# Rework of the Haar and mixer stages of a small vision tower: what VectorE, ScalarE and GpSimd each do

## The chip, the cores and the metric

The kernel runs on one core of one Trainium2 chip. The metric is the device time of one execution in microseconds: the median of three runs before the change is 135.28 us (134.98 to 137.23).

## The reference, cut to what matters

The input is eight images of 256 by 256 (fp32). Three blocks follow one another:

```python
# 1. wavelet block: three Haar levels down, weights, three levels up
cur = img
for _ in range(3):
    cur, h, v, d = _dwt2(cur); details.append((h, v, d))
rec = cur * sigmoid(cur.reshape(B, -1) @ Wa + ba)[:, :, None]
for (h, v, d), (Wd, bd) in zip(reversed(details), det_params):
    w = softmax(stack([h, v, d], 1).reshape(B, -1) @ Wd + bd)
    rec = _idwt2(rec, h * w[:, 0], v * w[:, 1], d * w[:, 2])
h = rec
# 2. mixer, on x = layernorm(h)
delta = softplus(x @ Wdelta + bdelta);  B_bar = delta * (x @ Wb + bb)
A_cum = clip(cumsum(delta * -softplus(A), axis=1), -20, 20)
state = exp(A_cum) * cumsum(B_bar * exp(-shifted(A_cum)), axis=1)
h = h + state @ Wc + bc + x @ Wd + bd
# 3. quantised FFN, on x = layernorm(h): 8-bit rounding by maxima of x, of each
#    weight row and of silu(gate) * up, which are taken over whole tensors
h = h + ffn(x)
```

## The kernel before, in words

The eight images form two halves of four. A half lies on 128 partitions (image and row strip) with eight rows of 256 on each. Every engine has its instructions in one order that is written out by hand; semaphores join them. There is no scheduler: an engine stands still at the first instruction whose wait isn't met, and all that is behind it stands too.

VectorE makes the Haar sums and differences of the first half (`analyse_level`, L898 for the step down the rows) and of the second (`down_second`). TensorE transposes the bands, makes the dots with the weights, and makes the logits of the softmax. `shifted_logits` and `band_weights` are a chain of tiny VectorE instructions around an exponential on ScalarE. `synthesise_level` goes up again, from level 2 to level 0: at each level four scaled sums (L974 and L977) make a column step out of average and horizontal, vertical and diagonal detail, and two sums (L981, L983) join them. ScalarE scales only the vertical detail (L740). Moments follow (L987), then row normalisation, shared by ScalarE (L770) and VectorE (L1002).

TensorE transposes the normalised rows; ScalarE copies them out of PSUM (L781); TensorE projects them (L540) and makes the direct part of the mixer (L556). ScalarE makes the softplus. VectorE makes the step sizes (L1042), a scan over time for the logarithmic decay (L1056, L1060), the state's input (L1049), then a product, a scan and a product for the state (L1066, L1067, L1070). GpSimd adds the mixer's biases once the state is there (L395). VectorE takes the maxima of the FFN's weights (L1027) and their scales between the states of the two halves; ScalarE rounds the weights (L749) and GpSimd clamps them. `keep_warm` matmuls on TensorE have no use but to keep it busy. VectorE then adds the mixer's result, normalises, takes the maximum of the whole tensor, and the FFN runs.

## Time and profile before

| What | Value |
|---|---|
| Median of the runs (range) | 135.28 us (134.98 to 137.23) |
| Profiled execution, its span | 135.05 us, 133.3 us |
| Busy: VectorE, TensorE, ScalarE, GpSimd | 119.4, 105.8, 74.5, 31.4 us |
| Chain that ended last: VectorE, TensorE, issue | 62%, 24%, 5% |
| Mean granted clock of TensorE | 0.947 |
| Haar stage, mixer, second normalisation and maximum, FFN (about) | to 46, to 68, to 85, to 133 us |

The profile comes from one execution. An instruction's duration is from its start to its end; independent instructions on one engine overlap by about a tenth of a microsecond, so a run of equal ones is shorter than count times duration. The chain that ended last is followed back from the last instruction: at each step to what released it. The granted clock is 1.00 for 2.4 GHz and 0.50 for 1.2 GHz.

### The profile page before, as it was taken

To read this page: it belongs to the slowest core of one execution; us is meant where nothing else is said; L and a number is where in the kernel's file an instruction comes from. 1 tells how busy PE (TensorE), PEld (TensorE's weight loads), DVE (VectorE), ACT (ScalarE), POOL (GpSimd) and SP (SyncE) were. 2 spreads that over 40 slices of the span, in tenths; PEclk is the share of its full clock that TensorE was granted. 3 is DMA by queue.
4 is the path that set the end of the run, shared out by engine and by line. 5 is a ranking of instruction groups with operands and counts; after the bars stand their busy time and mean duration, and the time that the engine had idled before them with its cause. 6 is when DMAs were issued, how large, how long until landed. Compare 5 with 4: busy or idle time off the path is not lost.

```text
span 133.3 us, 1778 instructions
## 1 busy us (share of the span) xinstructions
PE 105.8 (79%) x589; PEld 70.5 (53%) x589; DVE 119.4 (90%) x250; ACT 74.5 (56%) x145; POOL 31.4 (24%) x46
## 2 busy tenths in 40 slices
PE   0588979993989988799999329689999993996830
PEld 0577967993753856548889103144344331764410
DVE  0599978999979999999997999788999998999992
ACT  3204324421795139678943949369999921997000
POOL 6400000001000000490369700007767730000000
PEclk9999999999599999999999975799999999999995
DMA  3999950000000000000230390029000000003354
GB/s 87 362 421 306 417 224 7 0 0 0 0 0 0 7 0 0 0 0 0 50 68 5 76 163 0 0 46 174 17 0 0 7 0 0 0 33 125 121 194 157
DMA packets 10938, 10.21 MB, mean 77 GB/s; under 512 B 8370, under 2 KB 8626, under 8 KB 10802
## 3 DMA queue, kind: packets, MB, share of 16 engines
q1 hardware_dynamic: 10642, 9.59, 23.5%
q10 hardware_dynamic: 288, 0.52, 1.1%
q8 instruction: 4, 0.07, 0.2%
q14 instruction: 4, 0.03, 0.1%
HBM read 6.05 MB, written 2.10 MB: 61 GB/s over the span
## 4 chain that ended last, share of the span: by engine, by line
DVE 62%; PE 24%; issue 5%; DMA 3%; POOL 2%; ACT 2%; DVEq 0%
PE bank L608 13%; DVE stats L987 4%; DVE early L1208 4%; PE bank L427 4%; DVE state_mem L1204 4%; DVE wabs L1027 4%; DVE xmax L1084 3%; DVE middle L1197 3%; DVE early L977 3%; DVE early L974 3%; PE bank L487 3%; DVE h L1078 3%; DMA early<-in_x 3%; DVE middle L898 2%; POOL h L395 2%
## 5 line engine op out<-in xcount | busy, mean ns | idle before, releaser
L608 PE MATMUL bank<-state_mem,wqT 128*128 128x512 bf16 x80 | 17.7, 380 | 0.5 <-DVE state_mem L1163 0.5
L420 POOL TENSOR_TENSOR early<-raw,state_mem 128x512 f32<-128x512 f32 x10 | 13.0, 1296 | 19.1 <-ACT raw L871 19.1
L432 PE MATMUL bank<-restart,ident 128*128 128x512 bf16 x39 | 12.7, 472 | 4.8 <-DVE xmax L1084 4.8
L395 POOL TENSOR_TENSOR h<-h,bias_rows 128x512 f32<-128x512 f32 x8 | 9.9, 1274 | 24.7 <-DVE state_mem L1070 24.7
L864 ACT ACTIVATE state_mem<-bank,gscale 128x512 f32<-128x512 f32 x22 | 14.4, 700 | 1.1 <-PE bank L608 0.8
L621 PE MATMUL bank<-wqT,middle 128*128 128x256 bf16 (+1 forms) x96 | 12.6, 274 | 2.5 <-DVE middle L1197 2.4
L556 PE MATMUL bank<-mixer_w,early 128*128 128x256 f32 x64 | 14.5, 382 | 0.0
L1173 DVE TENSOR_REDUCE amax<-early 128x1 f32<-128x1024 f32 x11 | 13.2, 1212 | 0.4 <-POOL early L420 0.4
L556 PEld LDWEIGHTS bank<-mixer_w,early 128*128 128x128 f32 x64 | 11.9, 190 | 2.6 <-issue 1.1
L770 ACT ACTIVATE early<-h,nmr,rstd 128x256 f32<-128x256 f32 x23 | 11.9, 589 | 1.8 <-DVE nmr L995 1.8
L608 PEld LDWEIGHTS bank<-state_mem,wqT 128*128 128x128 bf16 x80 | 7.3, 98 | 10.5 <-DVE early L1181 1.8
L877 ACT ACTIVATE raw<-early,ainv 128x512 int16<-128x512 f32 x16 | 9.9, 710 | 5.0 <-DVE ainv L1193 5.0
L621 PEld LDWEIGHTS bank<-wqT,middle 128*128 128x128 bf16 (+1 forms) x96 | 8.3, 97 | 7.1 <-DVE middle L1197 4.4
L722 ACT ACTIVATE early<-bank 128x512 f32<-128x512 f32 x8 | 4.4, 598 | 12.2 <-PE bank L427 12.2
L987 DVE BATCH_NORM_STATS2 stats<-h 128x6 f32<-128x512 f32 x16 | 10.6, 695 | 0.3
L432 PEld LDWEIGHTS bank<-restart,ident 128*128 128x128 bf16 x39 | 4.4, 118 | 10.2 <-DVE xmax L1084 5.0
L487 PE MATMUL bank<-wT,early 128*128 128x96 f32 x48 | 9.2, 352 | 0.0
L1181 DVE SCALAR_TENSOR_TENSOR early<-bank,gscale,state_mem 128x512 f32<-128x512 f32 x12 | 8.9, 745 | 0.1
L649 PE MATMUL bank<-ident 128*128 128x128 f32 x20 | 4.6, 428 | 4.9 <-DMA early<-in_x 4.9
L540 PE MATMUL bank<-early,mixer_w 128*64 128x512 f32 x32 | 7.4, 599 | 1.2 <-ACT early L781 1.2
L487 PEld LDWEIGHTS bank<-wT,early 128*128 128x128 f32 x48 | 8.0, 205 | 0.1
L763 ACT ACTIVATE var<-stats,eps 128x8 f32<-128x8 f32 x4 | 1.2, 304 | 12.2 <-DVE stats L987 12.2
(144 smaller groups left out, 207.3 us busy)
## 6 DMA issues: line engine op xcount, KB each, us to landing
out<-early SPq DMA_DIRECT2D x7, 256.0 KB, 2.5
early<-in_x SPq DMA_DIRECT2D x1, 1024.0 KB, 8.9
wT<-in_dot_weights SPq DMA_DIRECT2D x1, 784.0 KB, 6.9
raw<-in_gate_rows SPq DMA_DIRECT2D x1, 768.0 KB, 11.1
raw<-in_up_rows SPq DMA_DIRECT2D x1, 768.0 KB, 12.4
raw<-in_down_rows SPq DMA_DIRECT2D x1, 768.0 KB, 13.7
early<-in_x ACTq DMA_DIRECT2D x2, 256.0 KB, 4.8
early<-in_x SPq DMA_DIRECT2D x2, 256.0 KB, 4.7
```

The costliest lines, as they stand in the source:

```text
L395: nc.gpsimd.tensor_tensor(rows, rows, bias.unsqueeze(1).to_broadcast([P, 2, C]), ALU.add).then_inc(biased, 1)
L420: nc.gpsimd.tensor_tensor(act[:, u, :], up_s[:, m % UPS, :], silu[:, u % SIL, :], ALU.mult).then_inc(pool_act_ready, 1)
L432: nc.tensor.matmul(into[:, :], ident16[:, :], restart[:, 0:PAIR // 2].bitcast(bf16), start=True, stop=True)
L487: nc.tensor.matmul(own(half, 0)[:, 0:3 * S], bandT[:, half, 4 * b + r, :], wT1[:, b, :, r::4], start=(m + r == 0), stop=(m == 2 and r == 3 ...
L556: nc.tensor.matmul(own(half, MIX[n])[:, i * C:(i + 1) * C], xnT[:, half, c, (2 * n + i) * P:(2 * n + i + 1) * P], wd_t[:, c, :], start=(i ...
L608: last = nc.tensor.matmul(dst[:, :], w, xqT[:, k, :, c, :], start=(c == 0), stop=(c == CH - 1))
L621: return nc.tensor.matmul(down_bank(n, i)[:, i * C:(i + 1) * C], act_q[rows, unit_of[t, k], q * P:(q + 1) * P], wdT[rows, t, :], start=sta ...
L770: nc.scalar.activation(xn[:, half, r, :], h[:, half, r, :], ACT.Identity, bias=nmr[:, norm, half, r:r + 1], scale=rstd[:, norm, half, r:r ...
L864: nc.scalar.activation(silu[:, u % SIL, :], bank[2 * (u % 3)][:, :], ACT.Silu, scale=gscale[:, 0, t:t + 1]).then_inc(silu_ready, 1)
L877: nc.scalar.activation(act_i[:, u, :], act[:, u, :], ACT.Copy, scale=ainv[:, :]).then_inc(acti_ready, 1)
L987: last = nc.vector.bn_stats(stats[:, norm, half, 2 * n:2 * n + 2, :].rearrange("p r k -> p (r k)"), h[:, half, 2 * n:2 * n + 2, :].rearran ...
L1173: nc.vector.tensor_reduce(amax[:, m:m + 1], act[:, 2 * m:2 * m + 2, :].rearrange("p a t -> p (a t)"), AX.X, ALU.max, apply_absolute_value= ...
```

## The change

It rewrites the first two blocks in several places and moves small pieces between engines.

- Sums of the analysis and of the second half's row step are joined or parted differently: one instruction covers both outputs of `down`, and the four sums of `down_second` stand in another order.
- The softmax chain is shorter: twelve logits with pads, the image weight's sign in the mask, no negated weights, the average scaled in one instruction. The small constants of the limits are made on GpSimd.
- At level 1 of both halves and level 0 of the second (`PRESCALED`), ScalarE scales the horizontal and diagonal details too; VectorE then makes the column step by one sum and one difference over both parts. At the other levels the four scaled sums stay, with the subtraction in the operator.
- On ScalarE the second half's small products stand ahead of the first two copies of transposed rows, and its level 0 products ahead of the last two.
- In the mixer the clipped sum comes from one scan per image with a limit, the decay is the exponential of its differences, and the state is a scan that adds and multiplies. Of the second half VectorE normalises four rows, not two, and copies two of four transposed tiles out of PSUM; ScalarE copies the others.
- Four `keep_warm` matmuls go, and the second half's transposes and projections stand ahead of the last direct bank.
- Of the weight scales VectorE keeps the reciprocal; GpSimd makes the rest, behind the first half's biases.
- The two quantisations of activations multiply by two scalars at once instead of making a scale first.

Core of the diff:

```diff
+        PRESCALED = ((1,), (1, 0))
...
+                pool.wait_ge(wabs_ready, 1)
+                nc.gpsimd.tensor_scalar(winv[:, :, :], wabs_inv[:, :, :], QMAX, None, ALU.mult).then_inc(winv_ready, 1)
+                nc.gpsimd.tensor_scalar(wscale[:, :, :], wabs[:, :, :], 1.0 / QMAX, None, ALU.mult).then_inc(wscale_ready, 1)
+                pool.wait_ge(wscale_ready, 1)
+                for c in range(CH):
+                    last = nc.gpsimd.tensor_scalar(diag[:, c, :], ident[:, :], wscale[:, 2, c:c + 1], None, ALU.mult)
+                last.then_inc(diag_ready, 1)
...
                 if half == 1:
+                    weight_scales()
                     clamp_weights(0)
                 add_bias(half)
...
             projections(0)
             mix_direct(0, (0, 1, 2))
-            keep_warm(WARM_PROJECT, own(1, 3))
-            xn_transposed(1, GROUPS[1][0])
+            for g in GROUPS[1]:
+                xn_transposed(1, g)
+            projections(1)
             mix_direct(0, (3,))
-            xn_transposed(1, GROUPS[1][1])
-            projections(1)
             mix_state(0, range(R // 2))
...
                 for n in levels:
-                    nc.scalar.activation(vband[n][:, half, :], band[n][:, half, V_, :], ACT.Copy,
-                                         scale=wts[:, half, 3 * n + 1:3 * n + 2]).then_inc(v_ready, 1)
+                    dst = vband2[:, half, :] if n == 2 else coarse[n][:, 1, :]
+                    nc.scalar.activation(dst, band[n][:, half, V_, :], ACT.Copy,
+                                         scale=wts[:, half, 3 * n + 1:3 * n + 2]).then_inc(v_ready[n], 1)
+                    if n in PRESCALED[half]:
+                        for k, b in ((0, H_), (1, D_)):
+                            nc.scalar.activation(detail[n][:, k, :], band[n][:, half, b, :], ACT.Copy,
+                                                 scale=wts[:, half, 3 * n + 2 * k:3 * n + 2 * k + 1]).then_inc(detail_ready[n], 1)
...
             def decays(half):
-                sc.wait_ge(alog_ready, half + 1)
-                v = lambda t: t[:, half, :].rearrange("p (a t) -> p a t", t=T)
-                nc.scalar.activation(v(edn)[:, :, 1:T], v(alog)[:, :, 0:T - 1], ACT.Exp, scale=-1.0).then_inc(edn_ready, 1)
-                nc.scalar.activation(eup[:, half, :], alog[:, half, :], ACT.Exp).then_inc(eup_ready, 1)
+                if half == 0:
+                    sc.wait_ge(acol_ready, 1)
+                sc.wait_ge(dlog_ready, half + 1)
+                nc.scalar.activation(decay[:, half, :], dlog[:, half, :], ACT.Exp,
+                                     scale=acol[:, 4:5]).then_inc(decay_ready, 1)
...
-            normalise(0, 0, range(ACT_ROWS[0] - 1))
+            normalise(0, 0, ACT_ROWS[0][:-1])
             softmax_exp(1)
-            normalise(0, 0, (ACT_ROWS[0] - 1,))
+            normalise(0, 0, ACT_ROWS[0][-1:])
+            scale_vertical(1, (2, 1))
             xn_out(0, (0,))
-            scale_vertical(1, (2, 1))
+            scale_vertical(1, (0,))
             xn_out(0, (1,))
-            scale_vertical(1, (0,))
             softplus(0)
             inverse_std(0, 1)
-            normalise(0, 1, range(R // 2))
+            normalise(0, 1, ACT_ROWS[1])
+            xn_out(1, (0, 1))
             decays(0)
-            normalise(0, 1, range(R // 2, ACT_ROWS[1]))
-            xn_out(1, (0, 1))
             softplus(1)
             quantise_weights(0)
...
-                vert = vband[n][:, half, :].rearrange("p (r c) -> p r c", c=width)
-                for odd, w in enumerate((wts, wneg)):
-                    stt(dst[:, 0, odd::2, :], bandv[:, H_, :, :], w[:, half, 3 * n:3 * n + 1], avg, ALU.mult, ALU.add)
-                dve.wait_ge(v_ready, 3 * half + 3 - n)
-                for odd, w in enumerate((wts, wneg)):
-                    step = seq.mark(stt(dst[:, 1, odd::2, :], bandv[:, D_, :, :], w[:, half, 3 * n + 2:3 * n + 3], vert,
-                                        ALU.mult, ALU.add))
+                if n in PRESCALED[half]:
+                    parts = coarse[n][:, :, :].rearrange("p k (r c) -> p k r c", c=width)
+                    details = detail[n].rearrange("p k (r c) -> p k r c", c=width)
+                    dve.wait_ge(v_ready[n], half + 1)
+                    dve.wait_ge(detail_ready[n], 2 * (half + 1 if n else half))
+                    tt(dst[:, :, 0::2, :], parts, details, ALU.add)
+                    step = seq.mark(tt(dst[:, :, 1::2, :], parts, details, ALU.subtract))
+                else:
+                    vert = (vband2[:, half, :] if n == 2 else coarse[n][:, 1, :]).rearrange("p (r c) -> p r c", c=width)
+                    for odd, op in enumerate((ALU.add, ALU.subtract)):
+                        stt(dst[:, 0, odd::2, :], bandv[:, H_, :, :], wts[:, half, 3 * n:3 * n + 1], avg, ALU.mult, op,
+                            reverse1=odd == 1)
+                    dve.wait_ge(v_ready[n], half + 1)
+                    for odd, op in enumerate((ALU.add, ALU.subtract)):
+                        step = seq.mark(stt(dst[:, 1, odd::2, :], bandv[:, D_, :, :], wts[:, half, 3 * n + 2:3 * n + 3], vert,
+                                            ALU.mult, op, reverse1=odd == 1))
...
+            def second_turned(m):
+                g = GROUPS[1][m]
+                dve.wait_ge(xnT_psum, 4 + 2 * m + CH)
+                nc.vector.tensor_copy(xnT[:, 1, CH - 1, 4 * g * P:4 * (g + 1) * P],
+                                      own(1, 2 * g + CH - 1)[:, :]).then_inc(xnT_ready, 1)
...
             def log_decay(half):
                 dve.wait_ge(delta_ready, half + 1)
-                seq.link(nc.vector.tensor_tensor_scan(csum[:, :], restart[:, :], delta[:, :], 0.0,
-                                                      ALU.mult, ALU.add))
                 if half == 0:
-                    dve.wait_ge(acol_ready, 1)
-                ts(alog[:, half, :], csum[:, :], acol[:, 4:5], -20.0, ALU.mult, ALU.max).then_inc(alog_ready, 1)
+                    dve.wait_ge(limit_ready, 1)
+                    dve.wait_ge(consts, 1)
+                for q in range(B // 2):
+                    step = seq.mark(nc.vector.tensor_tensor_scan(csum[:, q, 1:T + 1], delta[:, q * T:(q + 1) * T],
+                                                                 limit[:, 0:1].to_broadcast([P, T]), 0.0, ALU.add, ALU.min))
+                seq.wait(step)
+                tt(dlog[:, half, :].rearrange("p (q t) -> p q t", t=T), csum[:, :, 1:T + 1], csum[:, :, 0:T],
+                   ALU.subtract).then_inc(dlog_ready, 1)
             def state(half):
-                dve.wait_ge(edn_ready, half + 1)
+                dve.wait_ge(decay_ready, half + 1)
                 dve.wait_ge(bbar_ready, half + 1)
-                seq.link(tt(bsh[:, :], bbar[:, half, :], edn[:, half, :], ALU.mult))
-                seq.link(nc.vector.tensor_tensor_scan(hs[:, :], restart[:, :], bsh[:, :], 0.0,
-                                                      ALU.mult, ALU.add))
-                dve.wait_ge(eup_ready, half + 1)
-                tt(hT[:, half, :], eup[:, half, :], hs[:, :], ALU.mult).then_inc(hT_ready, 1)
+                for q in range(B // 2):
+                    cut = slice(q * T, (q + 1) * T)
+                    last = nc.vector.tensor_tensor_scan(hT[:, half, cut], bbar[:, half, cut], decay[:, half, cut], 0.0,
+                                                        ALU.add, ALU.mult)
+                last.then_inc(hT_ready, 1)
...
-            down_second(ALU.add, A_).then_inc(bands[1], 1)
+            down_second(ALU.add, A_, 0)
+            down_second(ALU.add, A_, 1).then_inc(bands[1], 1)
             own_strips(0)
-            down_second(ALU.subtract, H_).then_inc(bands[1], 1)
+            down_second(ALU.subtract, H_, 0)
             shifted_logits(0)
+            down_second(ALU.subtract, H_, 1).then_inc(bands[1], 1)
...
-            normalise_rows(0, 0, range(ACT_ROWS[0], R))
+            normalise_rows(0, 0, DVE_ROWS[0][:2])
             shifted_logits(1)
+            limits()
+            normalise_rows(0, 0, DVE_ROWS[0][2:])
...
             centre(0, 1)
+            normalise_rows(0, 1, DVE_ROWS[1])
+            state_input(0)
+            for m in range(2):
+                second_turned(m)
             log_decay(0)
-            state_input(0)
-            normalise_rows(0, 1, range(ACT_ROWS[1], R))
+            weight_maxima(0)
             state(0)
-            weight_maxima(0)
             weight_maxima(1)
```

Two places show the moved order. On ScalarE, from the second half's softmax to the softplus (`early<-bank` is the copy of transposed rows, the rows with `wts` are the scaled details), before:

```order
L734 ACTIVATE ez<-zc 128x10 [waits z_ready]
L770 ACTIVATE early<-h,nmr,rstd 128x256 [waits nmr_ready]
L781 ACTIVATE early<-bank 128x512 [waits xnT_psum] x2
L740 ACTIVATE middle<-middle,wts 128x32 [waits wts_ready]
L740 ACTIVATE middle<-middle,wts 128x128
L781 ACTIVATE early<-bank 128x512 [waits xnT_psum] x2
L740 ACTIVATE middle<-middle,wts 128x512 [waits wts_ready]
L790 ACTIVATE state_mem<-bank,cols 128x512 [waits proj_done]
```

and in the changed kernel:

```order
L767 ACTIVATE ez<-zc 128x12 [waits z_ready]
L808 ACTIVATE early<-h,nmr,rstd 128x256 [waits nmr_ready]
L774 ACTIVATE middle<-middle,wts 128x32 [waits wts_ready]
L774 ACTIVATE early<-middle,wts 128x128
L778 ACTIVATE early<-middle,wts 128x128 x2
L819 ACTIVATE early<-bank 128x512 [waits xnT_psum] x2
L774 ACTIVATE early<-middle,wts 128x512 [waits wts_ready]
L778 ACTIVATE early<-middle,wts 128x512 x2
L819 ACTIVATE early<-bank 128x512 [waits xnT_psum] x2
L828 ACTIVATE state_mem<-bank,cols 128x512 [waits proj_done]
```

Four products stand ahead of the first copies, three of 512 elements ahead of the last ones.

On VectorE, from the row normalisation of the second half to its step sizes (`state_mem` holds the mixer's tensors, `wabs` the weight maxima), before:

```order
L1002 TENSOR_SCALAR early<-h,rstd,nmr 128x256 x2
L1066 TENSOR_TENSOR state_mem<-state_mem 128x512
L1067 SCALAR_TENSOR_TENSOR state_mem<-restart,state_mem 128x512
L1070 TENSOR_TENSOR state_mem<-state_mem 128x512
L1027 TENSOR_REDUCE wabs<-raw 128x6 x2
L1027 TENSOR_REDUCE wabs<-raw 128x2
L1032 TENSOR_SCALAR wscale<-wabs 128x18
L1033 RECIPROCAL winv<-wscale 128x18
L1035 TENSOR_SCALAR diag<-ident,wscale 128x128 x2
L1042 TENSOR_TENSOR state_mem<-state_mem 128x512
```

and in the changed kernel:

```order
L1056 COPY early<-bank 128x512 x2
L1096 SCALAR_TENSOR_TENSOR state_mem<-state_mem,limit 128x256 x2
L1099 TENSOR_TENSOR state_mem<-state_mem 128x512
L1068 TENSOR_REDUCE wabs<-raw 128x6
L1108 SCALAR_TENSOR_TENSOR state_mem<-state_mem 128x256 x2
L1068 TENSOR_REDUCE wabs<-raw 128x6
L1068 TENSOR_REDUCE wabs<-raw 128x2
L1073 RECIPROCAL wabs_inv<-wabs 128x18
L1079 TENSOR_TENSOR state_mem<-state_mem 128x512
```

Two copies out of PSUM now stand ahead of the scans, one weight maximum stands between scans and state, and the scales are gone from VectorE. The scans read SCALAR_TENSOR_TENSOR in this listing.

## Rows read from the trace of the kernel before

**Rows 1.** Chain that ended last, shares of the span by engine.

```profile
DVE 62%; PE 24%; issue 5%; DMA 3%; POOL 2%; ACT 2%; DVEq 0%
```

**Rows 2.** Timeline of VectorE, 9 to 23 us: start, duration (us), instruction, [idle before].

```profile
9.09 1.43 DVE L898 TENSOR_TENSOR middle<-early 128x256 f32<-128x256 f32 x4
...
15.61 1.29 DVE L926 TENSOR_TENSOR middle<-early 128x512 f32<-128x512 f32 x2
...
17.75 0.49 DVE L936 TENSOR_TENSOR picked<-bank,strip_mask 128x320 f32<-128x320 f32 x1 [0.71 <-PE bank L498]
18.27 0.49 DVE L938 TENSOR_REDUCE part<-picked 128x10 f32<-128x320 f32 x1
...
20.84 0.18 DVE L958 RECIPROCAL rden<-den 128x4 f32<-128x4 f32 x1
...
22.98 0.35 DVE L974 SCALAR_TENSOR_TENSOR early<-middle,wts,early 128x128 f32<-128x128 f32 x1
```

**Rows 3.** Timeline of TensorE, the second matmul of the first half's logits.

```profile
19.20 0.39 PE L509 MATMUL bank<-bias,ones 1*128 1x10 f32 x2
```

**Rows 4.** Timeline of VectorE, 33 to 44 us.

```profile
33.04 0.49 DVE L938 TENSOR_REDUCE part<-picked 128x10 f32<-128x320 f32 x1
...
33.64 1.38 DVE L1002 TENSOR_SCALAR early<-h,rstd,nmr 128x256 f32<-128x256 f32 x4
...
37.11 0.25 DVE L974 SCALAR_TENSOR_TENSOR early<-middle,wts,avg 128x32 f32<-128x32 f32 x1
...
38.09 0.25 DVE L977 SCALAR_TENSOR_TENSOR early<-middle,wts 128x32 f32<-128x32 f32 x1 [0.57 <-ACT middle L740]
...
40.91 0.75 DVE L974 SCALAR_TENSOR_TENSOR early<-middle,wts,early 128x512 f32<-128x512 f32 x1
...
43.68 1.23 DVE L981 TENSOR_TENSOR h<-early 128x1024 f32<-128x1024 f32 x1
```

**Rows 5.** Timeline of ScalarE: vertical products, copies out of PSUM, weight rounding.

```profile
37.75 0.60 ACT L740 ACTIVATE middle<-middle,wts 128x32 f32<-128x32 f32 x2
38.25 1.07 ACT L781 ACTIVATE early<-bank 128x512 f32<-128x512 f32 x2
39.20 0.73 ACT L740 ACTIVATE middle<-middle,wts 128x512 f32<-128x512 f32 x1
...
60.41 2.51 ACT L749 ACTIVATE raw<-raw,winv 128x256 int16<-128x256 f32 x6 [0.34 <-DVE winv L1033]
```

**Rows 6.** Timeline of TensorE, 39 to 55 us: projections, direct part, transposes.

```profile
39.46 3.67 PE L540 MATMUL bank<-early,mixer_w 128*64 128x512 f32 x16 [0.45 <-ACT early L781]
43.07 5.45 PE L556 MATMUL bank<-mixer_w,early 128*128 128x256 f32 x24
...
53.85 1.04 PE L427 MATMUL bank<-ident,early 128*128 128x128 f32 x8
```

**Rows 7.** Windows of TensorE: stretch, length, busy (instructions), granted clock, DMA share, GB/s.

```profile
31.30:33.50 2.20, 0.00 (x1) 1.00 0.00 0
33.70:37.10 3.40, 3.40 (x15) 0.51 0.00 0
...
78.40:85.00 6.60, 5.75 (x14) 0.50 0.25 31
```

**Rows 8.** Timeline of VectorE in the mixer, 49 to 68 us.

```profile
49.27 1.22 DVE L1056 TENSOR_TENSOR_SCAN state_mem<-restart,state_mem 128x512 f32<-128x512 f32 x1
...
54.22 0.69 DVE L1070 TENSOR_TENSOR state_mem<-state_mem 128x512 f32<-128x512 f32 x1
54.82 4.93 DVE L1027 TENSOR_REDUCE wabs<-raw 128x6 f32<-128x1536 f32 x3
...
64.97 0.68 DVE L1066 TENSOR_TENSOR state_mem<-state_mem 128x512 f32<-128x512 f32 x1
...
66.94 0.69 DVE L1070 TENSOR_TENSOR state_mem<-state_mem 128x512 f32<-128x512 f32 x1
```

**Rows 9.** Timeline of GpSimd, the first half's bias.

```profile
55.08 4.96 POOL L395 TENSOR_TENSOR h<-h,bias_rows 128x512 f32<-128x512 f32 x4 [21.58 <-DVE state_mem L1070]
```

192 lines of the change are left out of this document (100 added, 92 removed).

## The prediction

> **What bounds the kernel now.** I read the chain of waits first: VectorE holds 62% of it [rows 1], so a VectorE instruction that goes away counts, unless the engine was about to wait there. Then the timeline of each engine around the change. In the Haar stage VectorE waits only twice: 0.71 us for the first half's dots and 0.57 us for ScalarE's scaled vertical detail [rows 2, 4]. From 38 to 67 us it runs without a gap while TensorE and ScalarE deliver ahead of it [rows 5, 6, 8]. The reader is to see that the cover is thin: TensorE's projections begin the moment ScalarE's last copy of the transposed rows ends [rows 5, 6], and what is queued on ScalarE ahead of those copies moves TensorE.
>
> **Stage 1, up to the first half's image.** The four 256-element sums of an analysis step take 1.43 us and two of 512 take 1.29 [rows 2]: 0.14 us less, twice before TensorE may start, once each at the two coarse levels. TensorE's chain starts 0.28 us sooner; the rest ends in the 0.71 us wait. From the strip sum (end 18.76) to level 1 (22.98) it is 4.22 us now [rows 2]. After: the sum ends at 18.48, the logits follow 0.83 us later as now [rows 2, 3], maximum, shift and latencies take 0.40, and the second half of the sums (0.61, half of the 1.29 pair) covers the exponential, up to 20.31. Four dependent tiny steps at about 0.18 each [rows 2] less overlap give 0.65, level 2 its old 1.17 (two tiers of small instructions that don't change): level 1 starts at 22.13, 0.85 sooner. There, two sums of 256 (0.79, from the 256-element pace of 0.34) replace four scaled sums (0.35 each less overlap, 1.17 [rows 2]): 0.38. ScalarE's four small products at 0.25 to 0.30 [rows 5] end near 21.9, before they are wanted; it was idle then. Together 1.23 us at the first half's image, and level 0, whose form is new only in the operator, follows at its old price.
>
> **Stage 2, the second half's image.** From the strip sum's end (33.53) to level 2 (37.11) it is 3.58 us [rows 4]. After, counted from 32.30: maximum and shift lie between two pairs of row normalisations, the exponential waits for ScalarE's third row (34.0), and the tiny steps start when the fourth VectorE row has passed; level 2 starts at 34.88, after 2.58: 1.00 us. The vertical product is no longer behind ScalarE's copies, so the 0.57 us wait and its latency go (0.66 with the step's own spacing), and level 1 gives 0.38 again. VectorE stands at level 0 at 37.64 instead of 40.91 [rows 4].
>
> Now ScalarE. From the weights (34.70): four small products, 1.1 us; two copies out of PSUM, 1.0; then the vertical, horizontal and diagonal products of 512 at 0.61 apart, the last 0.73 long [rows 5]. The last ends at 38.78. VectorE waits **1.14 us** for it. Two sums of 1024 (2.41, from 1.23 each less overlap) replace four scaled sums (2.77 [rows 4]): 0.36. The image is 3.27 - 1.14 + 0.36 = 2.5 us sooner, and moments with it.
>
> Here a rule speaks against the change. The row: 512 elements scaled on ScalarE take 0.73 us, the scaled sum on VectorE 0.75, adding included [rows 4, 5]; so at level 0 three ScalarE products save 0.36 us of VectorE and cost 1.14 of waiting, while at level 1 the same exchange is free because ScalarE has nothing else to do. The Trainium skill ("ScalarE: Activation LUTs", Rules for kernel authors) says multiplications belong on VectorE rather than ScalarE; by it alone every prescaled level would lose, by the rows only the widest does.
>
> **Stage 3, the mixer.** ScalarE's two last copies (1.07 [rows 5]) now end at 39.8 instead of 39.3. TensorE: projections 3.61 (39.46 to 43.07) and three direct banks, 5.45 less overlap [rows 6], to 48.7; then all sixteen transposes of the second half, 0.13 each: 50.75. The four keep-warm matmuls between are gone, which only lets the transposes follow directly. VectorE passes step sizes and centring at 46.8 (49.27 less 2.5 [rows 8]), its four rows (1.38 [rows 4]) and the state input (0.75) at 48.9, and must now copy the second channel half of both groups out of PSUM: it waits, in sum some **1.4 us**, and the last copy (0.6, below the 0.69 of a 512-element sum [rows 8]) ends at 51.35. Behind it queue the scans: two of 256 (half of 1.22 each [rows 8], 1.26 together) and a difference (0.69): 53.35. The exponential lies under the first weight maximum (a third of 4.93 [rows 8]); the new state is two scans, 1.27, in place of product, scan, product (2.66 [rows 8]). State 0 ends at 56.3, **1.4 us later** than now (54.91 [rows 8]), with one weight maximum done early.
>
> From there to state 1 VectorE needs 10.15 us now (54.82 to 64.97 [rows 8]). After: 1.65 less for that maximum, 0.6 less for weight scales given to GpSimd, 0.3 more because scans and difference take 1.98 and not 1.66: 8.2, so 64.5. GpSimd, however, comes to the scales only after adding the bias (4.96 [rows 9]) behind state 0: 61.45. Its 18-element scale shows nowhere; I take 0.3, bounds 0.1 and 0.7. Six weight tiles on ScalarE (2.51 [rows 5]) stand ahead of the second exponential (at most 0.73): 65.0. So state 1 waits 0.5 us and ends at 66.3 against 67.63 (66.94 plus 0.69 [rows 8]): 1.35 sooner. TensorE's second direct part is then still running, as now, and the transposes of the weights leave SP's queue up to 1.5 us later, long before the FFN uses them.
>
> The two quantisations each lose one dependent tiny step on VectorE (0.12 and 0.11). The twelve-wide logits, the memsets, the fourth mask, the limits on GpSimd at 17 us lie beside other work; if they did not, it would be tenths. **Sum: 1.6 us, 133.45** against the profiled execution's 135.05.
>
> **TensorE's clock.** That sum needs the full clock. After 2.2 us without work the clock stood at half for 3.4 us (33.7 to 37.1), and after a longer pause from 78.4 to 85.0 [rows 7]. The change shortens the first pause (31.0 to 32.35 instead of 33.58), but between the last keep-warm matmul (near 36.95) and projections at 39.8 opens a new one of 2.9 us, with nothing to fill it. I expect it to fall there once. At half clock 3.4 us do 1.7 us of work, so the price lies between 0 and 1.7; part of the low stretch may fall into the pause, so I take 1.0. VectorE waits for the transposes, so all of it passes on. **Forecast: 134.5 us.** The median of the runs shown, 135.28, is 0.23 above the profiled execution, which is within their spread; I leave the forecast there.
>
> **The rivals.**
> - *The clock holds.* For it: a shorter pause of 1 us earlier in the trace left it alone, and if it still falls at 33 us the keep-warm matmuls run longer and close the second pause. Against: 2.2 us sufficed once. Time 133.45, 0.8 either way.
> - *The clock stays low for long*, as from 78.4 to 85.0 [rows 7]. Place: projections and direct mixing of the first half. Price 3.3 us; it decides the sign from 1.6 us on. Time 136.8, slower than before. Against it: that stretch began after 4 us of pause, and the work here is dense.
> - *ScalarE is late at both levels.* If the small products come after the level-2 step in both halves, level 1 gains nothing (0.76), and if the 512-element products don't overlap, level 0 waits 0.36 more: 135.6 with the fall. For it: 0.25 us spacing has one row only; against: it has 0.6 us to spare in the first half. The rule of the Trainium skill named above points this way.
>
> **How the numbers follow.** Forecast 0.45 (133.9 to 135.2), clock holds 0.30, late ScalarE 0.12, long low clock 0.10, something unseen 0.03. The range 132.5 to 136.5 leaves out the low end of the second case and the top of the fourth. A difference under 2% (below 132.57 or above 137.99) is what a measurement of this kernel can't well tell from none. Only the clock case with a cheaper PSUM copy gets below: 0.14. Only the long low clock with a late GpSimd gets above: 0.04. Within: 0.82.
>
> **What would show it.** In the changed profile: level 1 as two sums under 0.45 us each without a wait; a wait of about 1 us on ScalarE's diagonal product before the second half's level 0; a pause of near 3 us before the projections, and the granted clock there; VectorE's PSUM copies waiting for TensorE; state 0 later and state 1 sooner than now; a short wait of state 1 for the exponential. I am wrong if VectorE's PSUM copies don't wait, or if the second state comes later than 67.6 us.

## The result, and the profile after

The change makes the kernel slower by 0.9%: 137.43 us (median of 20 executions, 135.7 to 141.68) against 136.76 us (20, 134.64 to 138.79) for the kernel before on the same chip. The ratio is 1.0094, with a 95% interval of 1.0056 to 1.0132. (The ratios here come from undisturbed executions alone, so they can differ a little from those of the medians, and four traces below, those without prescaled level 0 in the changed kernel, with the earlier rounding, with GpSimd's sums and without any prescaling, come from slower executions.) The forecast was 134.5 us, the range 132.5 to 136.5, and the sign was a gain of 0.6% on 135.28. The profiled execution took 135.96 us, its span 134.2 (before 135.05 and 133.3): 0.91 us more.

The chain that ended last, by engine, answers [rows 1]:

```profile
DVE 44%; PE 31%; ACT 8%; issue 7%; POOL 5%; DMA 3%; DVEq 0%; POOLq 0%
```

VectorE holds 44% of it and not 62%. TensorE has 31% and not 24%, ScalarE 8% and not 2%, GpSimd 5% and not 2%: more work that lay beside VectorE is now waited for.

**The Haar stage.** VectorE, from the first half's level 1 to the second half's moments, answers [rows 2, 4] (start, duration in us, instruction, idle before and who ended it):

```profile
22.01 0.42 DVE L1010 TENSOR_TENSOR early<-early 128x256 f32<-128x256 f32 x1
22.35 0.42 DVE L1011 TENSOR_TENSOR early<-early 128x256 f32<-128x256 f32 x1
...
35.17 0.41 DVE L1015 SCALAR_TENSOR_TENSOR early<-middle,wts,avg 128x32 f32<-128x32 f32 x2
...
39.06 1.23 DVE L1010 TENSOR_TENSOR early<-early 128x1024 f32<-128x1024 f32 x1 [1.17 <-ACT early L778]
...
43.90 2.51 DVE L1029 BATCH_NORM_STATS2 stats<-h 128x6 f32<-128x512 f32 x4
```

Level 1 starts at 22.01 (22.98 before) as two sums of 0.42 without a wait; the second half's level 2 at 35.17 (37.11). Level 0 waits 1.17 us for ScalarE's diagonal product. The moments end at 46.41, 2.17 us sooner than before. Of this 0.23 us is chance: the first sums of the images began at 4.58 us here and at 4.81 before, and in the other kernels below at 4.58 to 5.12, once at 6.33.

**TensorE's clock**, which answers [rows 7] (stretch, length, busy time and instructions of TensorE's matmuls, its weight loads, VectorE, ScalarE and GpSimd, then granted clock, DMA share, GB/s):

```profile
30.80:32.20 1.40, 0.00 (x0) 0.00 (x0) 1.36 (x4) 0.51 (x2) 0.72 (x1) 1.00 0.00 0
32.30:37.40 5.10, 5.10 (x22) 4.57 (x23) 4.52 (x21) 4.64 (x12) 0.00 (x0) 0.51 0.00 0
37.40:39.20 1.80, 1.80 (x6) 0.46 (x4) 0.63 (x3) 1.80 (x4) 0.00 (x0) 0.50 0.00 0
...
40.04:43.71 3.67, 3.67 (x17) 1.34 (x17) 3.64 (x4) 1.69 (x3) 0.00 (x0) 1.00 0.00 0
```

The clock fell after the pause of 1.46 us before 32.26, not at the projections. The transposes and keep-warm matmuls then ran at half clock to 39.36, and only 0.68 us was idle before the projections at 40.04, which ran at the full clock in the 3.67 us they had before.

**The mixer.** VectorE from the first half's step sizes (L1079) over the copies out of PSUM (L1056) to the state of the second half (L1108), answers [rows 8]:

```profile
46.32 0.68 DVE L1079 TENSOR_TENSOR state_mem<-state_mem 128x512 f32<-128x512 f32 x1
...
50.00 0.69 DVE L1056 COPY early<-bank 128x512 f32<-128x512 f32 x1 [0.73 <-PE bank L462]
50.88 0.69 DVE L1056 COPY early<-bank 128x512 f32<-128x512 f32 x1 [0.18 <-PE bank L462]
51.48 1.26 DVE L1096 TENSOR_TENSOR_SCAN state_mem<-state_mem,limit 128x256 f32<-128x256 f32 x2
...
55.05 1.26 DVE L1108 TENSOR_TENSOR_SCAN state_mem<-state_mem 128x256 f32<-128x256 f32 x2
...
59.70 1.07 DVE L1079 TENSOR_TENSOR state_mem<-state_mem 128x512 f32<-128x512 f32 x1
60.81 2.23 DVE L1096 TENSOR_TENSOR_SCAN state_mem<-state_mem,limit 128x256 f32<-128x256 f32 x2
...
65.72 2.03 DVE L1108 TENSOR_TENSOR_SCAN state_mem<-state_mem 128x256 f32<-128x256 f32 x2
```

The same three steps cost more in the second half than in the first: the step-size sum 1.07 against 0.68, the decay scans 2.23 against 1.26, the state scans 2.03 against 1.26: 2.1 us in all. State 0 ends at 56.31, state 1 at 67.75 (67.63 before): of the 2.17 us nothing is left. GpSimd in that stretch answers [rows 9]. The first row holds the third and fourth bias addition together, the second row the fourth alone:

```profile
58.95 2.95 POOL L419 TENSOR_TENSOR h<-h,bias_rows 128x512 f32<-128x512 f32 x2
60.17 1.73 POOL L419 TENSOR_TENSOR h<-h,bias_rows 128x512 f32<-128x512 f32 x1
...
61.99 0.55 POOL L425 TENSOR_SCALAR winv<-wabs_inv 128x18 f32<-128x18 f32 x1
62.51 0.60 POOL L426 TENSOR_SCALAR wscale<-wabs 128x18 f32<-128x18 f32 x1
63.21 1.61 POOL L429 TENSOR_SCALAR diag<-ident,wscale 128x128 f32<-128x128 f32 x2
65.16 1.47 POOL L436 TENSOR_SCALAR raw<-raw 128x1536 bf16<-128x1536 int16 x1 [0.34 <-ACT raw L787]
```

The fourth addition, 60.17 to 61.90, took 1.73 us; four took 4.96 before. VectorE's scans started in it at 60.81. The state scans started at 65.72 in the clamp of 65.16 to 66.63. Before the change the additions (55.08 to 60.04) lay beside VectorE's three weight maxima (54.82 to 59.75), which read one operand.

ScalarE in that stretch:

```profile
62.57 2.51 ACT L787 ACTIVATE raw<-raw,winv 128x256 int16<-128x256 f32 x6 [5.63 <-POOL winv L425]
64.98 0.71 ACT L839 ACTIVATE state_mem<-state_mem,acol 128x512 f32<-128x512 f32 x1
```

It rounds the weights (L787) once GpSimd's 18-element scale is there, and makes the exponential (L839) behind that. The exponential ended at 65.69, so state 1 couldn't have started before 65.69 even with quick decay scans.

**The last stage.** From the first rounding (85.20; 85.35 before) to the maximum of the products it is 26.60 us and not 26.04. VectorE and GpSimd there, of the changed kernel:

```profile
90.60 1.54 DVE L1206 TENSOR_SCALAR state_mem<-state_mem 128x1024 bf16<-128x1024 int16 x1
...
90.59 1.27 POOL L455 TENSOR_TENSOR early<-raw,state_mem 128x512 f32<-128x512 f32 x1 [14.70 <-ACT raw L909]
```

and of the kernel before:

```profile
90.64 0.43 DVE L1158 TENSOR_SCALAR state_mem<-state_mem 128x1024 bf16<-128x1024 int16 x1
...
90.68 1.51 POOL L420 TENSOR_TENSOR early<-raw,state_mem 128x512 f32<-128x512 f32 x1 [14.91 <-ACT raw L871]
```

The same two instructions meet. Whichever starts first, here by 0.01 and there by 0.04 us, keeps its time; the other is stretched. From the second rounding to the last sum it is 0.63 us longer too (18.93 against 18.30). Seven instructions that now multiply by two scalars take 0.54 and 0.41 us where they took 0.48 and 0.35, which makes 0.4; the other 0.2 is a wait for TensorE, which the run with one scalar explains below.

### The profile page after: what moved, and what is told of

Same layout as the page of the kernel before. It is cut to its first block, busy times and chain, and to the rows that moved or that the text cites. A ratio compares the mean times of both kernels' runs of the same rounds, so it can differ in the third digit from the quotient of the medians.

```text
span 134.2 us, 1765 instructions
## 1 busy us (share of the span) xinstructions
PE 106.5 (79%) x585; PEld 71.3 (53%) x585; DVE 119.3 (89%) x227; ACT 74.3 (55%) x146; POOL 35.6 (27%) x59
## 4 chain that ended last, share of the span: by engine, by line
DVE 44%; PE 31%; ACT 8%; issue 7%; POOL 5%; DMA 3%; DVEq 0%; POOLq 0%
PE bank L642 11%; DVE early L1255 4%; PE bank L590 4%; POOL h L419 4%; DVE state_mem L1251 4%; PE bank L462 4%; DVE h L1118 4%; DVE xmax L1124 3%; PE bank L655 3%; PE bank L522 3%; DVE stats L1029 3%; DMA early<-in_x 3%; PE bank L574 3%; DVE middle L935 2%; DVE middle L1244 2%
## 5 line engine op out<-in xcount | busy, mean ns | idle before, releaser
L467 PE MATMUL bank<-restart,ident 128*128 128x512 bf16 x35 | 12.0, 494 | 7.0 <-DVE xmax L1124 7.0
L419 POOL TENSOR_TENSOR h<-h,bias_rows 128x512 f32<-128x512 f32 x8 | 10.4, 1329 | 25.5 <-DVE state_mem L1108 25.5
L655 PE MATMUL bank<-wqT,middle 128*128 128x256 bf16 (+1 forms) x96 | 13.9, 297 | 1.7 <-DVE middle L1244 1.7
L655 PEld LDWEIGHTS bank<-wqT,middle 128*128 128x128 bf16 (+1 forms) x96 | 9.2, 105 | 6.7 <-DVE middle L1244 3.3
L808 ACT ACTIVATE early<-h,nmr,rstd 128x256 f32<-128x256 f32 x21 | 10.9, 589 | 1.8 <-DVE nmr L1037 1.8
L787 ACT ACTIVATE raw<-raw,winv 128x256 int16<-128x256 f32 x12 | 5.0, 495 | 5.6 <-POOL winv L425 5.6
```

Source lines behind the costliest of these rows:

```text
L419: nc.gpsimd.tensor_tensor(rows, rows, bias.unsqueeze(1).to_broadcast([P, 2, C]), ALU.add).then_inc(biased, 1)
L467: nc.tensor.matmul(into[:, :], ident16[:, :], restart[:, 0:PAIR // 2].bitcast(bf16), start=True, stop=True)
L655: return nc.tensor.matmul(down_bank(n, i)[:, i * C:(i + 1) * C], act_q[rows, unit_of[t, k], q * P:(q + 1) * P], wdT[rows, t, :], start=sta ...
L808: nc.scalar.activation(xn[:, half, r, :], h[:, half, r, :], ACT.Identity, bias=nmr[:, norm, half, r:r + 1], scale=rstd[:, norm, half, r:r ...
```

## The experiments

The theory: what was to be won is lost where GpSimd's work lies beside VectorE instructions that read two operands from SBUF (**A**). The first rival: the new scans are slow in the second half by themselves (**B**).

**The scales back on VectorE.**

```diff
-                    weight_scales()
...
+                seq.link(ts(wscale[:, :, :], wabs[:, :, :], 1.0 / QMAX, None, ALU.mult))
+                nc.vector.reciprocal(winv[:, :, :], wscale[:, :, :]).then_inc(winv_ready, 1)
+                for c in range(CH):
+                    last = ts(diag[:, c, :], ident[:, :], wscale[:, 2, c:c + 1], None, ALU.mult)
```

> The changed kernel with the weight scales back on VectorE (0.66 us more there), nothing else. Theory A, GpSimd and VectorE hinder each other when VectorE reads two SBUF operands: the second half's decay scans (2.23 us for two in the changed kernel, 1.26 in the first half) fall to between 1.3 and 1.8 us since only the end of the bias additions still lies beside them, the state scans (2.03) stay slow where the clamping of the gate weights reaches them and else fall to 1.26, and state 1 ends 0.6 to 1.2 us sooner than 67.75; 0.5 to 1.0 us off the time of the changed kernel. Theory B, the new scans are slow by themselves in the second half: they stay at 2.2 and 2.0 us, and the time rises by 0.5 us.

Measured: 137.62 us (6 executions), ratio 1.0156 [1.0001, 1.0312]. VectorE, then GpSimd:

```profile
59.40 0.72 DVE L1072 TENSOR_SCALAR wscale<-wabs 128x18 f32<-128x18 f32 x1
...
60.34 1.25 DVE L1075 TENSOR_SCALAR diag<-ident,wscale 128x128 f32<-128x128 f32 x2
...
62.22 1.27 DVE L1099 TENSOR_TENSOR_SCAN state_mem<-state_mem,limit 128x256 f32<-128x256 f32 x2
63.53 1.77 DVE L1102 TENSOR_TENSOR state_mem<-state_mem 128x512 f32<-128x512 f32 x1
...
67.21 1.26 DVE L1111 TENSOR_TENSOR_SCAN state_mem<-state_mem 128x256 f32<-128x256 f32 x2
...
56.36 4.95 POOL L419 TENSOR_TENSOR h<-h,bias_rows 128x512 f32<-128x512 f32 x4 [24.10 <-DVE state_mem L1111]
63.14 1.61 POOL L436 TENSOR_SCALAR raw<-raw 128x1536 bf16<-128x1536 int16 x1 [1.84 <-ACT raw L786]
```

The scans are back at 1.27 and 1.26, with GpSimd idle beside them: B falls. But the time didn't come back, which A had expected: other instructions came to lie beside GpSimd. The scale took 0.72 (0.28 in the kernel before), the diagonal 1.25 (0.39), the difference 1.77 (0.69), ending 0.55 us after the clamp. State 1 ended at 68.47. Moving the cause moved the victim. Scale and diagonal read one tensor and not two, so A is too narrow as it is worded.

**The collision put into the old kernel.** GpSimd gets six instructions of 128x320 with unused results behind its bias additions; VectorE's are untouched.

```diff
+                    pool.wait_ge(winv_ready, 1)
+                    for k in range(6):
+                        seq.link(nc.gpsimd.tensor_scalar(picked[:, k % 2, :, :].rearrange("p j s -> p (j s)"),
+                                                         restart[:, 0:NW * S], 0.5, None, ALU.mult))
                     clamp_weights(0)
```

> The kernel before the change, with one thing added: behind the first half's bias additions GpSimd multiplies the strip mask by 0.5 six times (128x320 each, results not used), from the moment the weight scales are there (about 60.4 us) until about 63 us, beside VectorE's step-size sum and scan of the second half, whose instructions stay as they were. Theory A (a VectorE instruction that reads two operands from SBUF is held up while GpSimd works): in the second half the step-size sum takes about 1.0 us instead of 0.68 or the old scan about 2 instead of 1.22, in all 1.0 us more; state 1 ends about 1 us later, near 68.6; time about 0.7 us over the kernel before, less what the clock's phase hides. Theory B (the scans with a limit are slow in the second half for a reason of their own, data or form): the old sum and scan keep 0.68 and 1.22, state 1 ends at 67.6, time unchanged.

The second version differs in GpSimd's instruction alone, a sum of two operands from SBUF in place of a product of one with a constant:

```diff
+                        seq.link(nc.gpsimd.tensor_tensor(picked[:, k % 2, :, :].rearrange("p j s -> p (j s)"),
+                                                         restart[:, 0:NW * S], restart[:, S:(NW + 1) * S], ALU.add))
```

> The kernel before the change, again with six GpSimd instructions of 128x320 added behind the first half's bias additions (results not used), but now sums of two operands from SBUF in place of products of one operand with a constant. With the products the second half's sum, scan and state grew by 0.5 us in all and not by 1.0. Theory A, second form (what holds VectorE is GpSimd's traffic on SBUF, and an instruction with two operands makes more of it): step-size sum 0.69 grows to about 1.0, the scan from 1.35 to about 2.0, product, scan and product of the state together by 0.5 to 1.0 if GpSimd still works then; state 1 ends at 69.0 to 69.5 and not at 68.05. Theory B, second form (only scans with a limit, with their third operand, are held): as with the products, state 1 at 68.0 to 68.2.

With products: 136.26 us (10), ratio 1.0016 [0.9963, 1.0068]. The two scans, and GpSimd:

```profile
61.28 1.35 DVE L1060 TENSOR_TENSOR_SCAN state_mem<-restart,state_mem 128x512 f32<-128x512 f32 x1
...
65.79 1.47 DVE L1071 TENSOR_TENSOR_SCAN state_mem<-restart,state_mem 128x512 f32<-128x512 f32 x1
...
60.53 7.53 POOL L414 TENSOR_SCALAR picked<-restart 128x320 f32<-128x320 f32 x6 [0.52 <-DVE winv L1037]
```

With sums: 139.75 us (4), ratio 1.0200 [1.0107, 1.0293]:

```profile
61.47 1.77 DVE L1060 TENSOR_TENSOR_SCAN state_mem<-restart,state_mem 128x512 f32<-128x512 f32 x1
63.28 0.91 DVE L1064 TENSOR_SCALAR state_mem<-state_mem,acol 128x512 f32<-128x512 f32 x1
...
66.10 1.24 DVE L1070 TENSOR_TENSOR state_mem<-state_mem 128x512 f32<-128x512 f32 x1
67.38 1.77 DVE L1071 TENSOR_TENSOR_SCAN state_mem<-restart,state_mem 128x512 f32<-128x512 f32 x1
69.19 1.77 DVE L1074 TENSOR_TENSOR state_mem<-state_mem 128x512 f32<-128x512 f32 x1
...
60.71 7.36 POOL L414 TENSOR_TENSOR picked<-restart 128x320 f32<-128x320 f32 x6 [0.50 <-DVE winv L1037]
68.15 2.26 POOL L402 TENSOR_SCALAR raw<-raw 128x1536 bf16<-128x1536 int16 x1
```

State 1 ends at 68.05 with the products and 70.96 with the sums, 67.63 without either. So the old scan and products, which the change doesn't touch, slow down beside GpSimd as well: the collision is shown in the old kernel, and B's second form (only scans with a limit) falls. But A's price was wrong by kind. GpSimd worked equally long in both (7.53 and 7.36 us), and the products with a constant cost VectorE 0.45 us where the sums cost 3.2, counted from the step-size sum, some of it (the last product, 1.77 for 0.69) beside the clamp that they pushed back to 68.15. Also wrong in detail: the step-size sum at 60.75 kept its 0.69, and the clip with a scalar, which reads one operand, did grow, from 0.49 to 0.91. State 1 came 1.5 us later than A had expected at most (69.5).

**The new order on VectorE, with the scales there too.** Scans fill the wait for TensorE's transposes, and the one-operand maxima lie beside the bias additions.

```diff
             state_input(0)
+            log_decay(0)
             for m in range(2):
                 second_turned(m)
-            log_decay(0)
-            weight_maxima(0)
             state(0)
+            weight_maxima(0)
             weight_maxima(1)
```

> The changed kernel with the weight scales back on VectorE (as in the first experiment) and VectorE's order in the mixer changed: the first half's step-decay scans stand ahead of the two copies out of PSUM, and all three weight maxima stand behind the first state. So the scans fill the wait for TensorE's transposes, and the maxima, which read one operand, lie beside GpSimd's bias additions. Theory A (GpSimd's work holds VectorE's two-operand instructions): state 0 ends near 53.7 instead of 56.3; the three maxima take 4.9 to 5.0 us; the scales again 0.28 and 0.39, the second half's sum 0.68, its scans 1.26; state 1 ends near 65.4 instead of 67.75; time about 2 us under the changed kernel, 135.0 to 135.7, that is 0.985 to 0.995 of the kernel before. Theory B (the second half's state is bound by something else: ScalarE's rounding of the weights, TensorE, or transfers): state 1 stays at 67 to 68 and the time with it.

Measured: 134.62 us (6; 133.34 to 136.38), ratio 0.9877 [0.9785, 0.9970].

```profile
52.61 1.27 DVE L1111 TENSOR_TENSOR_SCAN state_mem<-state_mem 128x256 f32<-128x256 f32 x2
53.80 4.91 DVE L1067 TENSOR_REDUCE wabs<-raw 128x6 f32<-128x1536 f32 x3
58.75 0.30 DVE L1072 TENSOR_SCALAR wscale<-wabs 128x18 f32<-128x18 f32 x1
...
59.57 0.68 DVE L1082 TENSOR_TENSOR state_mem<-state_mem 128x512 f32<-128x512 f32 x1
60.28 1.27 DVE L1099 TENSOR_TENSOR_SCAN state_mem<-state_mem,limit 128x256 f32<-128x256 f32 x2
...
64.20 1.25 DVE L1111 TENSOR_TENSOR_SCAN state_mem<-state_mem 128x256 f32<-128x256 f32 x2
...
54.05 4.96 POOL L419 TENSOR_TENSOR h<-h,bias_rows 128x512 f32<-128x512 f32 x4 [21.36 <-DVE state_mem L1111]
62.08 1.53 POOL L436 TENSOR_SCALAR raw<-raw 128x1536 bf16<-128x1536 int16 x1 [3.06 <-ACT raw L786]
```

Every VectorE row has its unstretched price, GpSimd's additions 4.96. State 0 ends at 53.88 (expected 53.7), state 1 at 65.45 (65.4; 67.75 in the changed kernel). A holds in its numbers, but the new order does two things. From the moments to state 1 it takes 18.75 us and not 21.34: 2.1 us come from the rows that are no longer stretched, 0.9 from VectorE's waits for the copies, which are gone, and the scales take 0.6 of it back. So the collision is the larger part of what is won here, not all of it.

**Level 0 of the second half without prescaling**, in the changed kernel:

```diff
-        PRESCALED = ((1,), (1, 0))
+        PRESCALED = ((1,), (1,))
```

> The changed kernel without the prescaled details at level 0 of the second half: VectorE makes four scaled sums there again, ScalarE two products of 512 fewer. By the prediction's arithmetic the wait of 1.17 us goes and 0.36 us of VectorE's work comes back: the second half's image 0.8 us sooner, the projections 1.2 us sooner, state 0 at 55.2 to 55.6 instead of 56.3. How much arrives at the end depends on the mixer: 0.8 us if GpSimd's work moves along with state 0, near nothing if TensorE or the clash behind state 0 takes it.

Measured: 135.91 us (12), ratio 1.0004 [0.9929, 1.0080]; the changed kernel has 1.0094, and the intervals overlap. The collision is the same here (step-size sum 1.07, scans 2.23 and 2.03). Counted from the end of the strip sum, the moments end at 13.18 us and not 14.21, state 1 at 34.12 and not 35.55. Level 0 went without a wait through four scaled sums (1.42 and 1.41 for two). So prescaling at the widest level loses 1.0 us there and 1.4 at state 1. In the repaired kernel (new order, scales on VectorE, one scalar, below) the same edit was run again, and then prescaling taken out at level 1 as well (`PRESCALED = ((), ())`):

> As the one before, and level 0 of the second half by four scaled sums again, so that ScalarE scales horizontal and diagonal details at level 1 alone. State 1 ends 0.9 us sooner, near 64.5 (65.35 to 64.48 between the two kernels with all repairs). If the wait in the last stage that ate this there (1.26 us for ScalarE's gate, behind TensorE at half clock) came from the clock's phase, 0.5 to 0.9 us under the one before, about 132.5 to 133.5; if it comes whenever that stage starts sooner, no difference.

> The kernel with the new order, the scales on VectorE, one scalar, and no prescaling at any level: ScalarE scales the vertical details alone, and every column step is four scaled sums. Against the same kernel with level 1 prescaled (first half's level 1 at 22.39 us and two sums of 0.42 each, span 130.3; state 1 ends at 64.50). Theory A (the exchange gains at level 1, where ScalarE has nothing else to do): level 1 takes 1.17 in place of 0.79 in both halves, so the first half's image comes 0.38 later, the second half's 0.76 less what the second half's dots cover; state 1 ends at 65.0 to 65.3; time 0.4 to 0.8 over that kernel, 133.0 to 134.2. Theory B (prescaling is worth nothing at any level, as a rule that keeps products on VectorE would have it): the vertical products come sooner on ScalarE because four others are gone, level 0 and level 1 start sooner or at once, and state 1 ends at 64.5 or earlier.

| Prescaled levels, repaired kernel | Median (executions) | Ratio to before | State 1 ends |
|---|---|---|---|
| 1, and 0 of the second half | 134.80 us (6) | 0.9822 [0.9746, 0.9899] | 65.30 |
| 1 alone | 133.88 us (6) | 0.9831 [0.9759, 0.9903] | 64.51 |
| none | 135.01 us (6) | 0.9818 [0.9678, 0.9959] | 64.84 |

The ratios don't tell the three apart; the traces do. With level 0 prescaled VectorE waits 1.17 us at 39.22; without, it starts at 38.10 and state 1 comes 0.79 sooner; the two profiled executions took 132.91 and 132.06 us. At level 1, VectorE without and with prescaling (the first half's level 2 began 0.38 us later in the second of these executions):

```profile
36.49 0.61 DVE L1014 SCALAR_TENSOR_TENSOR early<-middle,wts,early 128x128 f32<-128x128 f32 x2
37.02 0.61 DVE L1018 SCALAR_TENSOR_TENSOR early<-middle,wts,early 128x128 f32<-128x128 f32 x2
```

```profile
36.50 0.43 DVE L1009 TENSOR_TENSOR early<-early 128x256 f32<-128x256 f32 x1
36.84 0.42 DVE L1010 TENSOR_TENSOR early<-early 128x256 f32<-128x256 f32 x1
```

Four scaled sums reach the row step 1.18 us after their start (36.49 to 37.67), two sums 0.79 (36.50 to 37.29). State 1 ended at 64.84, between what theory A (65.0 to 65.3) and theory B (64.5 or earlier) had expected. It is 0.33 later without prescaling although its first half began 0.38 earlier: together 0.7 for both halves, near the 0.76 of the expectation, provided that the earlier start would have reached the end. So level 1 gains 0.39 us in each half by these rows, and nothing of it can be seen in the time.

**One scalar in the quantisations.** The scale is made first, and one scalar multiplies:

```diff
-                    seq.link(ts(xq_i[:, half, rows, :], xn[:, half, rows, :], gmax1_inv[:, 0:1], limit_den[:, 1:2],
-                                ALU.mult, ALU.mult))
+                    seq.link(ts(xq_i[:, half, rows, :], xn[:, half, rows, :], xinv[:, 0:1], None, ALU.mult))
...
-                    rounded[u] = seq.mark(ts(act_i[:, u, :], act[:, u, :], amax1_inv[:, 0:1], limit_den[:, 2:3], ALU.mult, ALU.mult))
+                    rounded[u] = seq.mark(ts(act_i[:, u, :], act[:, u, :], ainv[:, 0:1], None, ALU.mult))
```

> The changed kernel with both quantisations multiplying by one finished scale again. Theory C, a tensor-scalar instruction with two pointer scalars costs 0.06 us more than with one, and seven of them in the last stage stand on the chain: roundings of 512 elements fall from 0.54 to 0.48 us, and 0.3 to 0.4 us go from the last stage; VectorE's clamp of the third block goes back from 1.54 to 0.43 us if it starts ahead of GpSimd's first multiplication, which takes another 0.4 us. In all 0.4 to 0.8 us faster than the changed kernel. Rival: the saved tiny step is worth more than that, and the time rises by 0.1 to 0.2 us.

Measured: 136.77 us (12), ratio 1.0079 [1.0025, 1.0133], not to be told from 1.0094. In the trace the roundings take 0.75 and 0.48 again, the clamp misses GpSimd's multiplication (0.43), and the first rounding to the maximum is 26.04 us as before the change (26.60 with it). From the second rounding to the last sum it is 18.72 and not 18.93; before 18.30. It isn't back at 18.30 because VectorE waited 0.28 us for TensorE's first product there, at granted clock 0.50 (115 to 118 us). The changed kernel had 0.50 there as well (114.3 to 117.6), and so had both old kernels with added GpSimd work; the old kernel by itself had 1.00. Two kernels with two scalars and a clock of 1.00 there (the scales on VectorE, and level 0 without prescaling) took 18.73: the second scalar costs 0.43 us, and the clock 0.2 more in the changed kernel's trace. In the repaired kernel:

> The kernel with the new order and the scales on VectorE, and the two quantisations multiplying by one scalar; the fourth quarter's rounding at its old place. From the pair without and with one scalar: seven roundings at 0.06 us, 0.3 to 0.5 us under the kernel with the new order alone (133.3 to 134.9 in its undisturbed executions), so 133.0 to 134.5; and if the earlier rounding is worth nothing, equal to the kernel with all repairs (132.8 and 133.0) within 0.5.

Measured: see the first row of the table; with two scalars the ratio was 0.9877, so the gain has the expected sign and lies within the intervals.

**The fourth rounding earlier**, so that no clamp meets the multiplication: `quantise_input(3)` stands behind `quantise_input(2)`, not behind the first product.

> The changed kernel with the last block's rounding and clamp placed ahead of the first product of the FFN, so that no VectorE clamp begins within GpSimd's first multiplication. Theory D, the clamp that took 1.54 us stood behind GpSimd's multiplication: no clamp over 0.5 us, the maximum over all units is reached 0.4 to 0.6 us sooner, 0.3 to 0.6 us off the time. Rival: the first product is late by 1.2 us instead, TensorE waits for its bank, and nothing is won.

Measured: 137.60 us (12), ratio 1.0056 [0.9998, 1.0115]. Inconclusive: the clamp is at 0.43 again, but VectorE then waited 1.60 us for ScalarE's gate (the silu of the FFN's products), with TensorE at granted clock 0.50 from 80 to 85 us in that execution. From the first rounding to the maximum it took 27.80 us. Two kernels without the earlier rounding had the clock at 0.50 in that stretch too and took nearly as long (new order 27.54, no prescaling 27.67).

**All repairs together**, with level 0 prescaled and without:

> As the kernel with the new order, and besides: the two quantisations multiply by one scalar that is made first, and the fourth quarter's rounding stands ahead of the first gated product. Theory A: the seven roundings on the last stage's path cost 0.06 us less each, about 0.4 in all, and the clamp that lay beside GpSimd's multiplication takes 0.43 instead of 1.54, about 0.4 us on the path at most; time 0.4 to 0.8 under the kernel with the new order alone. Theory B (the last stage is bound by TensorE at half clock and by the transfers, so VectorE's part doesn't pass through): within 0.3 us of the kernel with the new order alone.

> As the kernel with all three repairs, and besides level 0 of the second half by four scaled sums again, so that ScalarE scales horizontal and diagonal details at level 1 alone. Theory A (the exchange loses at the widest level, because VectorE waits 1.17 us for ScalarE's three products of 512 and saves 0.36): the moments end 1.0 us sooner than in the kernel with all repairs, state 1 near 64.3, time 0.5 to 1.4 us under that kernel, near 134.0, 0.98 of the kernel before. Theory B (the wait at level 0 stands where TensorE or the clock would be waited for anyway, now that the scans fill the wait): state 1 and time equal to the kernel with all repairs within 0.4 us.

Measured: 135.53 us (6; 132.76 to 136.11), ratio 0.9790 [0.9675, 0.9905], and 134.27 us (6; 131.81 to 135.08), ratio 0.9796 [0.9685, 0.9907]. State 1 ends at 65.38 and 64.51. That 0.87 us was lost again in the second profile: VectorE waited 1.26 us for ScalarE's gate, after TensorE's granted clock had been 0.50 from 84 to 87 us; in the first it was 1.00 there. Against the kernel without the earlier rounding (0.9822) the earlier rounding is worth nothing that can be measured; at clock 1.00 the stretch took 25.96 us with it and 26.04 without. Each of the six kernels with the new order beats both kernels, by 1 to 2% against before; which of them is best isn't settled.

## Why the prediction was wrong

The median, 137.43 us, lies above the range, and the kernel got slower where I had forecast a gain. About half of the distance to 134.5 is the base: the kernel before had 135.28 from three executions when I forecast and 136.76 from twenty. The rest is the change. In the profiled executions, which the working is about, it is 135.96 against 135.05; that this lies within the range is luck, since 1.0 us set aside for the clock wasn't needed and paid for part of what follows.

- **Stages 1 and 2: right in mechanism, with luck in the numbers.** Level 1 at 22.01 (22.13), no wait at level 1, 1.17 us of wait at level 0 (1.14), moments at 46.41 (46.08). Each of these times holds 0.23 us of the early start, which is luck. Level 2 of the second half came 2.97 us after the strip sum and not 2.58 (35.17, not 34.88), and VectorE stood 0.29 us for TensorE's logits there, at granted clock 0.51.
- **PSUM copies and state 0: right, in part by misses that cancel.** The copies waited 0.73 and 0.18 us, 0.9 and not 1.4, because VectorE itself came 0.4 us later than I had it; state 0 ended at 56.31 (56.3).
- **The step that failed: "From there to state 1".** I took GpSimd's additions and scales as work beside VectorE at prices from rows where each lay beside other work, to be paid for only in a wait of 0.5 us for the exponential. State 1 was to end at 66.3 and ended at 67.75, past my own sign of being wrong (67.6). My road to it ran over GpSimd and ScalarE, and the trace's chain goes that way too: the additions took 5.41 and not 4.96, the 18-element scale 0.55 and not 0.3, so the exponential ended at 65.69 and not 65.0; the state scans then took 2.03 and not 1.27. These three make the 1.45. VectorE's own road, 8.2 us from state 0 on, cost 0.38 more at the step-size sum and 0.97 at the decay scans, which used up the wait: both roads reached the state at 65.7. Moving the decay scans behind the copies, and one maximum ahead of state 0, took the one-operand work away from GpSimd's stretch; rows 8 and 9 side by side showed the old fit.
- **The two quantisations: wrong sign.** I booked 0.23 us for two tiny steps gone, and both came in (85.20 against 85.35; 1.18 us and not 1.30 from the maximum to the second rounding). But seven instructions cost 0.06 us more in the last stage and three before it, and the timing moved a clamp into GpSimd's multiplication. From 85.20 to the maximum 0.56 us was lost; from the second rounding to the end 0.63, of which 0.43 is the second scalar and 0.2 TensorE's clock.
- **TensorE's clock: the 1.0 us came in neither case.** The clock fell near 33 us, so the keep-warm matmuls ran long and closed the second pause, as the rival "the clock holds" gave for its second reason. The kernel with the scales on VectorE shows the other case: its clock stayed at 1.00 from 30 to 70 us, the keep-warm matmuls ended at 36.74, and the pause that I had feared opened, 3.18 us long. The projections behind it still took 3.68 us at clock 1.00. With that rival's 133.45 the sum was 2.5 us short of 135.96: 1.45 at state 1, 0.56 and 0.63 in the last stage, less 0.15 more than booked in between.
- **The other rivals:** ScalarE was not late at level 1, and no long low stretch came between 40 and 60 us. "Slower than before" came by a mechanism that stood in none of them.
- **The rule of the Trainium skill weighed there** ("ScalarE: Activation LUTs", Rules for kernel authors) fits level 0, where the products on ScalarE made VectorE wait, and not level 1, where they saved 0.39 us a half. A page of the Trainium skill that bears on the failed step was left out of the prediction. The Trainium skill ("SBUF — State Buffer", Who interferes with whom) says that a VectorE instruction with two SBUF inputs, or in a two-port mode, and a GpSimd instruction that reads SBUF exclude each other, and that whichever issues first holds the ports for its whole length. Most rows agree: in the changed kernel the first decay scan ended 0.55 us after the fourth addition and the state's first scan 0.54 after the clamp (at 62.45 and 67.17), near the 0.6 that one scan takes without a neighbour; the one-operand maxima were never held (4.91 to 4.93). No run here shows which VectorE instructions are in such a mode; it is where the clamp and the scales would have to belong. GpSimd's products with a constant don't agree: they read SBUF too, and held the scans by 0.13 and 0.24 us alone.

## What to carry to other kernels

Before moving work, list for each stretch what GpSimd does and which VectorE instructions run beside it: here the maxima, the moments and the sums that read PSUM kept their prices there (0.70 to 0.72 us for moments of 512 elements, 0.66 to 0.68 for sums, beside additions), while sums and scans of two SBUF operands, and the scales, clips and clamps of one, were stretched. A repair that only moves GpSimd's work moves the victim; reorder so that the right kind of VectorE work meets it. Sharing a product out to another engine pays only at the width at which that engine is done before it is waited for.

## What the runs showed of the hardware

- VectorE's instructions stretched beside GpSimd, both with operands in SBUF: a sum of 512 elements 0.69 to 1.77 us, two scans 1.26 to 2.23, a clamp 0.43 to 1.54, a clip 0.49 to 0.91, a scale of 18 elements 0.28 to 0.72. GpSimd is held as well: an addition 1.27 to 1.73, a clamp 1.47 to 2.26.
- The kind of GpSimd's instruction decides: six sums of two operands cost VectorE 3.2 us, six products of one operand with a constant, as long on GpSimd, 0.45. The number of operands isn't the whole of it: GpSimd's clamp reads one tensor too, from int16 to bf16, and stretched the state's two scans from 1.26 to 2.03. Why is not shown.
- A second scalar operand costs VectorE 0.06 us an instruction (0.48 to 0.54 for 512 elements, 0.75 to 0.81 for 1024).
- A pause alone doesn't tell whether TensorE's clock falls: near 31 us it fell after 1.46 us in the changed kernel and stayed at 1.00 after 1.46 and 3.18 us with the scales on VectorE, and after 1.83 us without prescaling.
- TensorE's clock goes with more time in the last stage than any single repair of it is worth. From the first rounding to the maximum six kernels whose clock was 1.00 in the 5 us behind the rounding took 25.96 to 26.12 us, unless a clamp was stretched (26.60); five whose clock was 0.50 in part or all of it took 27.45 to 27.80.
